# The quantiser of the second product ahead of the tail: one call moved in a software-pipelined feed-forward loop

## The reference, cut to what matters

```
def act_quant(x):
    scale = 127.0 / clip(max(abs(x), axis=-1), EPS)
    return clip(round(x * scale), -128, 127), scale
def weight_quant(w):
    scale = 1.0 / clip(mean(abs(w)), EPS)
    return clip(round(w * scale), -1, 1), scale
def qlinear(x, w, b):
    xq, sx = act_quant(x)
    wq, sw = weight_quant(w)
    return einsum('bsd,hd->bsh', xq, wq) / (sx * sw) + b
def ffn(x):
    h = gelu(qlinear(layernorm(x, gamma, beta), w1, b1))    # 1024 -> 4096
    return qlinear(h, w2, b2)                               # 4096 -> 1024
x = x + layernorm(linear_attention(layernorm(x), W_qkv, W_o))
x = x + layernorm(ffn(layernorm(x)))
```

## Time and profile before

| | |
|---|---|
| median of 5 runs | 3533.33 us (3519.79 to 3582.39) |
| the profiled execution | 3533.33 us |
| its span, slowest core (core 6) | 3531.8 us (the 8 cores: 3492.4 to 3531.8) |
| mean granted TensorE clock | 0.772 to 0.778 of full speed |
| busy shares: TensorE, VectorE, ScalarE, GpSimd | 60%, 44%, 21%, 4% |
| FFN parts of the four segments, first matmul | 777.2, 1559.95, 2340.57, 3118.04 us |

### The profile page before, as it was taken

One profiled execution on the slowest core, in us unless ns is written; L12 is line 12 of the kernel. 1 busy time (PEld: TensorE's weight loads), 2 busy tenths in 40 slices (PEclk: granted clock), 3 DMA queues, 4 the chain that ended last, 5 costly groups with the idle time before them and its releaser, 6 DMA issues.

```text
span 3531.8 us, 33855 instructions; the slowest of 8 cores (3492.4 to 3531.8 us)
## 1 busy us (share of the span) xinstructions
PE 2108.2 (60%) x10604; PEld 1040.8 (29%) x10640; DVE 1538.5 (44%) x2492; ACT 724.3 (21%) x1193; POOL 145.0 (4%) x203
## 2 busy tenths in 40 slices
PE   0061576747667367746866377647676366657665
PEld 0050444413222134412322144413222243313222
DVE  0575634345543143445553134455452244355442
ACT  0030312212222012212221122222221122122221
POOL 0141300000000000000000000000000000000000
PEclk9999566669888666768887667668888676678887
DMA  9797901131221411131121311131112311031111
GB/s 188 242 193 238 199 19 34 27 104 27 42 42 25 136 28 28 25 106 35 33 42 39 125 28 24 28 113 36 28 35 39 128 26 35 24 108 33 42 32 40
DMA packets 333137, 245.50 MB, mean 70 GB/s; under 512 B 304272, under 2 KB 304288, under 8 KB 328864
## 3 DMA queue, kind: packets, MB, share of 16 engines
q0 software_dynamic: 97440, 184.58, 19.3%
q1 hardware_dynamic: 235520, 58.74, 9.1%
HBM read 159.41 MB, written 33.55 MB: 55 GB/s over the span
## 4 chain that ended last, share of the span: by engine, by line
PE 41%; DMA 20%; DVE 20%; ACT 8%; issue 7%; DVEq 1%; another core or an unknown queue 0%; SPq 0%; ACTq 0%; POOLq 0%; POOL 0%; PEldq 0%; PEld 0%
PE pb L988 14%; PE pb L906 13%; DMA abf<-abf 6%; PE pb L492 6%; DMA af<-x 5%; DMA af<-w 4%; PE pb L499 3%; DMA w2q_t<-w2qs 3%; PE pb L909 2%; DMA wqkv_t<-w_qkv 1%; DVE abf L576 1%; DVE af L569 1%; DMA out<-x 1%; ACT af L1029 1%; DVE x L1034 1%
## 5 line engine op out<-in xcount | busy, mean ns | idle before, releaser
L906 PE MATMUL pb<-w1q_t,abf 128*128 128x512 fp8e4 x2048 | 541.1, 412 | 390.0 <-DMA abf<-abf 330.2
L988 PE MATMUL pb<-w2q_t,abf 128*128 128x512 fp8e4 x2048 | 497.8, 406 | 78.0 <-ACT s2rowr L977 44.3
L906 PEld LDWEIGHTS pb<-w1q_t,abf 128*128 128x128 bf16 x2048 | 190.6, 103 | 667.1 <-issue 510.9
L492 PE MATMUL pb<-abf,wqkv_t 128*128 128x128 bf16 x2048 | 196.9, 288 | 260.1 <-DMA abf<-abf 260.1
L988 PEld LDWEIGHTS pb<-w2q_t,abf 128*128 128x128 bf16 x2048 | 206.8, 103 | 351.4 <-issue 151.5
L492 PEld LDWEIGHTS pb<-abf,wqkv_t 128*128 128x128 bf16 x2048 | 192.2, 136 | 264.0 <-issue 264.0
L921 DVE TENSOR_REDUCE khs<-af 128x1 f32<-128x1024 f32 x128 | 156.1, 1220 | 177.6 <-ACT af L917 114.3
L528 DVE TENSOR_REDUCE khs<-pb 128x8 f32<-128x512 f32 x32 | 22.1, 692 | 437.4 <-ACT af L509 437.4
L1021 DVE RECIPROCAL scal<-scal 128x1 f32<-128x1 f32 x32 | 5.2, 164 | 472.3 <-ACT scal L1017 472.3
L917 ACT ACTIVATE af<-pb,scal 128x512 f32<-128x512 f32 x256 | 161.3, 684 | 228.1 <-PE pb L909 227.3
L1001 ACT ACTIVATE af<-pb,scal 128x512 f32<-128x512 f32 x32 | 22.0, 687 | 559.4 <-PE pb L992 559.4
(11 more groups left out here) (162 smaller groups left out, 2754.5 us busy)
## 6 DMA issues: line engine op xcount, KB each, us to landing
af<-w POOLq DMA_DIRECT2D x16, 2048.0 KB, 10.0
wqkv_t<-qkvs POOLq DMA_DIRECT2D x3, 6144.0 KB, 24.4
af<-w POOLq DMA_DIRECT2D x32, 512.0 KB, 5.4
af<-w POOLq DMA_DIRECT2D x16, 1024.0 KB, 9.7
af<-x POOLq DMA_DIRECT2D x32, 512.0 KB, 3.9
w1q_t<-w1qs POOLq DMA_DIRECT2D x4, 4096.0 KB, 16.3
w2q_t<-w2qs POOLq DMA_DIRECT2D x4, 4096.0 KB, 26.7
out<-x POOLq DMA_DIRECT2D x32, 512.0 KB, 2.9
```

The lines of the kernel that those rows point to most:

```text
L492: mi = PE.matmul(pq, lhsT=wqkv[:, kk, m * 128:(m + 1) * 128], rhs=hf[:, kk, :], start=(kk == 0), stop=(kk == 7))
L906: PE.matmul(Bk[bb0 + n2][:, :], lhsT=xf[:, kk, :], rhs=w1q[:, kk, hs0:hs0 + 512], start=(kk == 0), stop=False)
L988: mi = PE.matmul(Bk[4 + n2][:, :], lhsT=xq2_fm[:, kk, :], rhs=w2q[:, kk, n2 * 512:n2 * 512 + 512], start=(kk == 0), stop=False)
```

## The change

One call moves. `f_q2` of a tile was called in the round of that tile, between `f_front_tp(gg + 1)` and `f_front(gg + 2)`, so behind the tail of tile `gg - 2` (the last call of the round before) on VectorE's queue, and behind the transpose of `xq1_tm` of the next tile on SyncE's. Now it is called one round earlier, between `f_f2(gg)` and `f_tail(gg - 1)`; that of tile 0 is called right after `f_f1(0)`. No instruction is added or left out, and the functions stay as they are.

```
         f_f1(0)
+        f_q2(0)
         for gg in range(G):
             if gg + 1 < G:
                 f_front_tp(gg + 1)
-            f_q2(gg)
             if gg + 2 < G:
                 f_front(gg + 2)
             if gg + 1 < G:
                 f_f1(gg + 1)
             f_f2(gg)
+            if gg + 1 < G:
+                f_q2(gg + 1)
             if gg >= 1:
                 f_tail(gg - 1)
         f_tail(G - 1)
```

## The result

The changed kernel takes 3554.19 us in the median of 43 runs (3540.08 to 3576.11), the kernel before 3533.4 us in 80 runs (3514.05 to 3582.39): ratio 1.006, 95% interval 1.0048 to 1.0072. It is slower by 21 us. Forecast was 3553 us.

What follows compares the result with a forecast made beforehand. No engine is full; order and waits set the time. Per segment +16.8 us at the start, -11.4 at the end, -0.5 in steady rounds: +4.9, over four segments +20 us on 3533.33, so 3553 us, range 3532 to 3568.

Steps and rivals of the forecast that it cites:

- The quantiser is covered behind P2's start: Steady round: the quantiser takes 8.8 us, and VectorE stood idle for 16.7 us behind P2's start, so it is covered.
- P2: Second product of a tile in the FFN part (f_f2) on TensorE; the number in brackets is the tile.
- X2b: Second of two DMAs transposing the quantiser's output, on SyncE's queue; forecast 4.3 us, 1.4 us to spare before the residual add ends.
- F: The moment P2 of a tile ends; F+4.9 means 4.9 us after it.
- P1: First product of a tile in the FFN part (f_f1) on TensorE; forecast to start at F+13.4 in steady rounds, as before.
- The start: Start of a segment: loss of 16.8 us, from P1(1) behind quantiser and transposes, P1(2)'s wait for X2b(1), and its cold start.
- The end: End of a segment: P2(7) starts at F+5.3 after P2(6) instead of 16.7 us, released by s2row; gain 11.4 us a segment.
- The steady round gains 0.1 us: Five steady rounds per segment: the next tile's front comes earlier, gaining 0.1 us a round, 0.5 us a segment.
- P2(7): Second product of a segment's last tile: cold start before and after; the bounds said it may save up to 1.0 us.
- The doubtful wait: Rival, steady rounds: the output DMA waits for an X2b of 7.7 us, +2 us in 20 rounds, 3593 us; chance 0.05.
- faster by the clock: Rival: P2 restarts at 2.4 instead of 1.2 GHz, 24 x 1.7 = 41 us come back, 3512 us; chance 0.08.

Runs made afterwards that it cites:

- X2b twice: Changed kernel with the second transpose of each tile's quantiser output issued twice, timed against the kernel before: 3628.78 us, ratio 1.027.
- X1 first in all rounds: Changed kernel with the transpose of the first product's input called right behind f_f2, ahead of quantiser transposes and tail, every round: 3285.77 us, ratio 0.930 to before.
- the swap: TensorE's waits for the previous evacuation and for s2row exchanged ahead of the second product: changed kernel 3509.69 us, kernel before 3486.43 us.
- the run without the output wait: Changed kernel, input transposes of tiles 3 to 7 not waiting for GpSimd's DMAs, including the tail's output DMA: 3444.61 us, ratio 0.9748 to the kernel before.

## Why the prediction was right

Point by point. *The quantiser is covered behind P2's start*: it runs from 1722.00 to 1730.77 in the round shown, P2(2) from 1720.93 to 1737.33. *X2b 0.56 us after P2's end, landing at F+4.9, the output DMA at F+7.0 and P1 at F+13.4 as before*: 0.53, 4.3 us later, 7.0 and 13.4; doubling X2b showed the cover, 1.5 us against 1.4. *The start*: +16.8 us forecast, +16.7 to +17.7 measured (17.1 in the mean: 8.0 for P1(1), 6.7 for the wait of P1(2), 2.4 for its cold start, where 7.9, 6.6 and 2.3 were forecast), with the gaps 20.7 (20.5 to 20.9 measured) and 8.3 (8.3 to 8.7), and P2(0) still warm at 14.7 us; its parts were taken back one at a time. *The end*: 11.4 us forecast, 11.4 to 12.2 measured, released by s2row. *The steady round gains 0.1 us*: here the term was mis-sized. The waits for the gelu are gone (no entry for it is left), and with the same gaps P1 is 3.3 us shorter in the 20 rounds. But the five rounds came out at +0.4 us a segment and not -0.5, since all 24 P2 restart at 1.2 GHz where 3 of 24 did not before: 3 x 1.7 = 5 us, which covers the gain. *P2(7)* was costed at no change and went from 17.0 to 17.4 us before to 16.0 to 17.6 after, +0.4 us in sum. *The doubtful wait*: where the prediction prices an X2b of 7.7 us, its 2 us count from the end of the residual add (F+6.3) and not from the output DMA (F+7.0), as X2b twice showed. The terms add up to +23.7 us in the FFN parts; the rest of the program came out 2.5 us shorter, which is little beside the 3540 to 3576 us of single runs. That the forecast is within 1 us of the median is luck: the two large terms are right to 1.2 us over the four segments, but the small misses (+3.6 us in the rounds, +0.4 in P2(7), -2.5 in the rest) happened to cancel in part.

The rival "faster by the clock" named a real price. The reason against it, that the idle time stays 1.60 us because no instruction between P1 and P2 moves, held for the idle time but doesn't decide alone: P2 kept its clock after 1.60 us in 3 of 24 cases before and in 17 of 24 with X1 first in all rounds. And the price was there to be had, with either order of the quantiser, by two waits changing place.

## What to carry to other kernels

Moving a block of work ahead on one engine moves its DMAs ahead on their queue too: list what they now stand ahead of, and what each of them waits for. Here the block itself was worth 11 us a segment in one round of eight, was hidden in the others, and its transposes cost 17 us in the first two, because a transpose that nobody needed yet stood ahead of one that TensorE was waiting for. A steady gap that several engines cross in turn (evacuate, normalise, add, store, transpose) is shortened by calling the urgent transfer first, not by taking work out of it that lies beside it; and the wait that ends last belongs behind those that are already met.

## What the runs showed of the hardware that was not expected

A satisfied wait on TensorE (its semaphore has long been reached) behind the one that ends last costs 0.11 us (idle 1.60 against 1.49 us ahead of P2), and at this place that decided about the clock: after 1.49 us 92 of 92 starts stayed at 2.4 GHz on the slowest cores (28 in each of the two kernels with the swap, 4 in each of nine others), after 1.60 us 7 to 24 of 24 fell to 1.2 GHz, at 1.7 us each. It is worth 1.2% of this kernel's time (0.9876). These are the slowest cores. Over all eight cores 734 of 736 starts after 1.49 us stayed, among them 294 behind a P1 of over 19.07 us; after 1.60 us 1584 of 1952 fell, and of those behind an unstalled P1 from a cold start just the ones whose P1 took over 19.07 us. So the idle time and how late the clock had risen in the product before both have a part. Why, was not settled.

The two starts that fell after the shorter gap lie in the run without the output wait, in a stretch in which the granted clock went between 0.50 and 0.81. Four cores of one die were granted 0.81 in that run, for 140 to 174 us each, and no core in any other profile.
